# Router logits from extra columns of the qkv and out layers, norm3 no longer turned, out in halves, new step numbers

## The reference

```python
# x [64, 32, 512], ctx [64, 257, 512], 16 heads of 32
x = x + xattn(_layernorm(x), ctx)          # softmax attention over 257 rows, then @ W_out.T + b_out
x = x + attn(_layernorm(x))                # q, k, v by low-rank layers with a rotation, 32 x 32 per batch, then @ Wo_w + Wo_b
x = x + ffn(_layernorm(x))

def ffn(x):                                # E = 8 experts, H = I = 512
    logits = xf @ Wg + bg
    idx = argmax(softmax(logits))
    h = gelu(einsum('th,ehi->tei', xf, W1) + b1)
    y = einsum('tei,eih->teh', h, W2) + b2
    return y[token, idx[token]]
```

## Time and profile before

| | |
|---|---|
| median of 3 runs | 849.17 us |
| profiled execution | 850.44 us |
| its span | 848.6 us |
| busy share | PE 88%, DVE 69%, ACT 52%, POOL 38% |
| first part with batches | to about 606 us |
| tail, to the first gather of the expert part | about 606 to 665 us |
| expert part | about 665 to 848.6 us |

### The profile page before, as it was taken

The page is one execution under the profiler, slowest core; times in us unless marked ns, Lnnn a source line. Parts: engine busy times, 40 slices in busy tenths (PEclk is TensorE's granted clock), DMA queues, the critical chain, the costliest instruction groups (busy, mean ns, idle before and its releaser), DMA issues.

```text
span 848.6 us, 26125 instructions
## 1 busy us (share of the span) xinstructions
PE 745.6 (88%) x10442; PEld 552.9 (65%) x10442; DVE 584.1 (69%) x1163; ACT 440.4 (52%) x1095; POOL 323.7 (38%) x638
## 2 busy tenths in 40 slices
PE   5997878989899898988989889898888779999998
PEld 3544756768677685776857667586676646666664
DVE  3467677777767777777777777767535646788883
ACT  2343475564655656556465655646422335555552
POOL 2113453342523424243242432424310444876642
PEclk9998999999899999999999999999998899999999
DMA  9953764665645565465654546442231599554430
GB/s 275 325 151 67 152 158 122 153 149 115 169 115 139 146 144 145 130 152 137 151 139 137 152 120 168 140 114 89 92 133 51 180 372 363 171 161 141 145 114 4
DMA packets 113848, 129.05 MB, mean 152 GB/s; under 512 B 13950, under 2 KB 80766, under 8 KB 113728
## 3 DMA queue, kind: packets, MB, share of 16 engines
q1 hardware_dynamic: 105984, 109.26, 46.8%
q0 software_dynamic: 5520, 16.26, 5.6%
q10 hardware_dynamic: 2224, 1.86, 0.8%
HBM read 114.76 MB, written 14.42 MB: 152 GB/s over the span
## 4 chain that ended last, share of the span: by engine, by line
PE 66%; DVE 9%; POOL 8%; ACT 7%; issue 6%; DMA 4%; SPq 0%; DVEq 0%; POOLq 0%; ACTq 0%
PE bank L507 11%; PE bank L509 9%; PE bank L508 9%; PE bank L1561 7%; PE scores L548 5%; PE bank L572 5%; PE bank L501 4%; PE scores L558 3%; ACT prob L823 3%; POOL operand_lo L1293 2%; PE bank L704 2%; PE scores L1539 2%; PE scores L1541 2%; PE scores L1540 2%; DMA k_block<-in_L_attn_Wu_v_w 2%
## 5 line engine op out<-in xcount | busy, mean ns | idle before, releaser
L823 ACT ACTIVATE prob<-scores,negmax 128x257 f32<-128x257 f32 x256 | 118.2, 477 | 26.4 <-DVE negmax L1031 25.7
L507 PE MATMUL bank<-qkv_hi,operand_hi 128*128 128x396 f32 x256 | 96.0, 375 | 0.0
L1031 DVE TENSOR_REDUCE negmax<-scores 128x2 f32<-128x514 f32 x128 | 82.0, 682 | 15.5 <-PE scores L548 15.5
L1021 DVE STREAM_TRANSPOSE k_t<-keys 128x512 f32<-128x512 f32 x128 | 87.8, 689 | 2.9 <-DMA keys<-in_ctx 2.9
L508 PE MATMUL bank<-qkv_lo,operand_hi 128*128 128x396 f32 x256 | 88.5, 346 | 0.0
L509 PE MATMUL bank<-qkv_hi,operand_lo 128*128 128x396 f32 x256 | 88.0, 344 | 0.0
L1561 PE MATMUL bank<-w_all,hidden 128*128 x184 | 82.8, 593 | 0.6 <-ACT hidden L1614 0.6
L572 PEld LDWEIGHTS bank<-prob_t,context 128*32 128x32 f32 x4096 | 46.6, 115 | 54.1 <-issue 46.6
L558 PE MATMUL scores<-consts,prob 128*128 128x128 f32 x512 | 74.8, 278 | 4.8 <-ACT prob L823 4.7
L1275 POOL COPY plast<-prob 128x2 f32<-128x2 f32 x128 | 24.7, 193 | 129.8 <-ACT prob L823 129.7
L1657 DVE TENSOR_TENSOR w_lo<-w_all,w_hi 128x512 fp32r<-128x512 f32 x89 | 71.6, 863 | 1.8 <-ACT w_hi L1593 1.7
(11 more groups left out here) (244 smaller groups left out, 1671.4 us busy)
## 6 DMA issues: line engine op xcount, KB each, us to landing
keys<-in_ctx SPq DMA_DIRECT2D x256, 128.0 KB, 4.4
context<-in_ctx SPq DMA_DIRECT2D x64, 512.0 KB, 4.6
w_all<-in_L_ffn_W SPq DMA_DIRECT2D x16, 1024.0 KB, 12.1
b<-in_L_ffn_b SPq DMA_DIRECT2D x23, 256.0 KB, 3.5
norm_scratch<-norm SPq DMA_DIRECT2D x16, 256.0 KB, 2.0
x_tile<-in_x SPq DMA_DIRECT2D x8, 256.0 KB, 5.5
x_pair<-in_x SPq DMA_DIRECT2D x8, 256.0 KB, 5.5
x_scratch<-x_tile SPq DMA_DIRECT2D x8, 256.0 KB, 3.0
```

Source lines behind the costliest of these rows:

```text
L507: pe.matmul(to, op_hi[op][:, c, :], w_hi[name][:, c, columns], start=(c == 0), stop=False)
L823: act.activation(prob[pair][:, gg, :], scores[:, g, 0:J], ACT.Exp, bias=negmax[b % 2][:, g:g + 1], accum_out=sums[t % 2][:, g, bl:bl + 1]) ...
L1021: dve.transpose(dst, src).then_inc(keys_turned, 1)
L1031: dve.tensor_reduce(negmax[b % 2][:, 2 * pair:2 * pair + 2], scores[:, 2 * pair:2 * pair + 2, 0:J], AX.X, ALU.max, negate=True).then_inc(m ...
```

## The change

- The layer norm before the router is folded: the router's weights are centred (their mean over the inputs taken off), so that a logit is (x2 @ centred Wg) / std + bg. x2 is x1 plus the out layer, and x1 @ centred Wg is the second norm's product times its std. So the qkv layer gets 8 columns more (`GATE_AT`, 398 in place of 396 per product), the out layer 8 more (Wo @ centred Wg).
- 520 columns do not fit a bank of 512, so out goes in two halves of 260 columns in two banks (`out_part`): 24 products in place of 12.
- TURN3, X3_MOVE and GATE are gone. CHOOSE starts from `gate_sum` (DVE, 8 columns, ahead of X2) and `rstd_r`. POOL gets three small operations per tile (`std_s`, `gate_x1` twice).
- Six set-up units are new: `center`, four `turned` (Wo turned) and `gate`.
- Nearly all step numbers are new, some banks too.

```diff
-AV, SELF_HI, SELF_LO, OUT, X2, ROOT3 = 66, 66, 70, (81, 85, 86, 87), 89, 85
-SCALE3, TURN3, X3_MOVE, GATE, CHOOSE, RANK, RANKED = 90, 95, 96, 105, 105, 120, 120
+AV, SELF_HI, SELF_LO, OUT, X2, ROOT3 = 63, 73, 71, (86, 88, 92, 94), 96, 99
+SCALE3, CHOOSE, RANK, RANKED = 104, 104, 120, 118
+GATE_KEEP = 43
...
-LATER = {'OUT': (16, -4), 'X2': (19, 0), 'SCALE3': (26, 12), 'TURN3': (29, 7), 'GATE': (38, 14), 'CHOOSE': (31, 4), 'RANK': (25, 1)}
+LATER = {'OUT': (11, -11), 'X2': (2, -3), 'SCALE3': (20, 12), 'CHOOSE': (11, 14), 'RANK': (26, -7)}
...
-QKV_W = 3 * D + ROT
+GATE_AT = 3 * D + ROT
+QKV_W = GATE_AT + E
...
+        def out_part(c):
+            hi, lo = out_weights(w_hi, c), out_weights(w_lo, c)
+            for half in range(2):
+                pe.matmul(out_pair[:, half, 0:HALF + GH], op_hi[OP_SELF][:, c, :], hi[:, half, :], start=(c == 0), stop=False)
+            for half in range(2):
+                pe.matmul(out_pair[:, half, 0:HALF + GH], op_hi[OP_SELF][:, c, :], lo[:, half, :], start=False, stop=False)
+            for half in range(2):
+                done = pe.matmul(out_pair[:, half, 0:HALF + GH], op_lo[OP_SELF][:, c, :], hi[:, half, :], start=False, stop=(c == G - 1))
+            return done
...
+            if kind == "center":
...
+                for g in range(G):
+                    done = pe.matmul(bank[:, 0:E], tables[:, P:2 * P], wg[:, g, :], start=(g == 0), stop=(g == G - 1))
+            if kind == "turned":
...
+                for k in range(G):
+                    done = pe.transpose(bank[:, k * P:(k + 1) * P], staged_a[:, k, c * P:(c + 1) * P], ident)
+            if kind == "gate":
...
+                for o in range(G):
+                    for k in range(G):
+                        pe.matmul(bank[:, o * E:(o + 1) * E], wo_t[:, k, o * P:(o + 1) * P], wg[:, k, :], start=(k == 0), stop=(k == G - 1))
+                for k in range(G):
+                    done = pe.matmul(bank[:, G * E:(G + 1) * E], tables[:, P:2 * P], wg_bias[:, k, :], start=(k == 0), stop=(k == G - 1))
...
-                done = dense_part(OP_SELF, c, "out", slice(0, D), bank)
+                done = out_part(c)
...
-            t = tile_at(step, TURN3, LATER["TURN3"])
-            if t >= 0:
-                bank = bank_for("norm3", t)
-                until.wait_ge(normed_r, t + 1)
-                turn(norm3, bank, norm3_turned)
-            t = tile_at(step, GATE, LATER["GATE"])
...
-                    done = pe.matmul(bank[:, 0:E], x3[:, g * P:(g + 1) * P], wg[:, g, :], start=(g == 0), stop=(g == G - 1))
...
+                until.wait_ge(gate_kept, t + 1)
+                until.wait_ge(gate_used, t)
+                dve.tensor_tensor(halves(gate_sum[:, :]), halves(gate_x1[t % 2][:, :]), out_pair[:, :, HALF:HALF + GH], ALU.add)
+                dve.tensor_tensor(halves(x_tile[t % 4][:, :]), halves(x_tile[t % 4][:, :]), out_pair[:, :, 0:HALF], ALU.add).then_inc(x2_made, 1)
...
-                dve.tensor_tensor(logits[:, :], banks[bank_of["gate"]][:, 0:E], bias_g[:, :], ALU.add).then_inc(gate_used, 1)
+                dve.scalar_tensor_tensor(logits[:, :], gate_sum[:, :], rstd["r"][:, :], bias_g[:, :], ALU.mult, ALU.add).then_inc(gate_used, 1)
```

More of the change, by code:

```diff
@@ L222, in program @@
     last_t, last_p = sba("last_t", [P, G, B]), sba("last_p", [P, G, B])
-    bias_xout, bias_out, bias_v = (sba(n, [P, D]) for n in ("bias_xout", "bias_out", "bias_v"))
+    bias_xout, bias_out = (sba(n, [P, D]) for n in ("bias_xout", "bias_out"))
+    bias_v = sba("bias_v", [P, D + E])
     bias_qk = sba("bias_qk", [P, 2, D])
     bias_g = sba("bias_g", [P, E])
-    wg = sba("wg", [P, G, E])
-    widths = (("xout", D), ("qkv", QKV_W), ("out", D))
+    wg, wg_bias, out_bias = sba("wg", [P, G, E]), sba("wg_bias", [P, G, E]), sba("out_bias", [P, G])
+    gate_c, gate_sum, std_s = sba("gate_c", [P, E]), sba("gate_sum", [P, E]), sba("std_s", [P, 1])
+    gate_x1 = [sba(f"gate_x1_{i}", [P, E]) for i in range(2)]
+    widths = (("xout", D), ("qkv", QKV_W), ("out", D + E))
     w_hi = {n: sba(f"{n}_hi", [P, G, w], F32R) for n, w in widths}
@@ L232, in program @@
     norm_x, norm_w, norm3 = (sba(n, [P, D]) for n in ("norm_x", "norm_w", "norm3"))
-    soft, x3 = sba("soft", [P, D]), sba("norm3_t", [P, D])
+    soft = sba("soft", [P, D])
     qk = sba("qk", [P, 2, D])
[L236 to L239, removed]
+    late = sba("late", [P, 6 * D + 2 * E])
+    att_w, soft_t, q2_t = (late[:, i * D:(i + 1) * D] for i in range(3))
+    v_w = [late[:, i:i + D + E] for i in (3 * D, 4 * D + E)]
+    last_w = late[:, 5 * D + 2 * E:6 * D + 2 * E]
     k_block = sba("k_block", [P, G, BT, HL, S])
@@ L385, in program @@
     emptied = {"queries": queries_placed, "xout": x1_made, "norm": norm_lo, "q": q2_moved, "self": soft_shifted, "av": self_lo,
-               "out": x2_made, "norm3": x3_moved, "gate": gate_used, "rank": rank_used}
+               "out0": x2_made, "out1": x2_made, "rank": rank_used}
     last_bank = banks[(bank_of["queries"] + 1) % 3]
@@ L516, in bank_for @@
             elif t == 0:
-                until.wait_ge(bias_moved, 4)
-                until.wait_ge(weight_lo, CUTS.index(("v", G - 1)) + 1)
+                for n in range(len(UNITS) - 3, len(UNITS)):
+                    until.wait_ge(*emptied_unit(n))
             if before is not None:
@@ L808, in set_up @@
                 cut(w_hi["qkv"][:, c, K_AT:K_AT + D], staged_d[:, c, :])
+            if kind == "turned":
+                until.wait_ge(unit_done, n + 1)
+                act.activation(wo_t[:, c, :], bank[:, :], ACT.Copy).then_inc(wo_turned, 1)
+            if kind == "gate":
+                until.wait_ge(unit_done, n + 1)
+                cut(gate_columns(w_hi), bank[:, 0:G * E].rearrange("p (c h e) -> p c h e", c=G, h=2))
         def move_prob(b, pair):
@@ L949, in scalar_program @@
                 until.wait_ge(staged_a_loaded, 32)
-                cut(w_hi["out"][:, step - OUT_CUT_AT, :], staged_a[:, step - OUT_CUT_AT, :])
+                cut(out_weights(w_hi, step - OUT_CUT_AT)[:, :, 0:HALF], halves(staged_a[:, step - OUT_CUT_AT, :]))
+            if step == GATE_CUT_AT:
+                until.wait_ge(centered, 1)
+                cut(w_hi["qkv"][:, :, GATE_AT:QKV_W], wg[:, :, :])
             stages(step)
@@ L1318, in stages @@
             if t >= 0:
+                until.wait_ge(gate_used, t)
                 root("r", measured_r, t + 1, normed_r, rstd_r)
+            t = tile_at(step, GATE_KEEP)
+            if t >= 0:
+                until.wait_ge(qkv_moved, 4 * t + 4)
+                until.wait_ge(x2_made, t - 1)
+                until.wait_ge(weight_lo, len(CUTS))
+                until.wait_ge(pool_own, own.count)
+                a = own.done(pool.tensor_scalar(gate_x1[t % 2][:, :], v_w[t % 2][:, D:D + E], std_s[:, :], None, ALU.mult))
+                until.wait_ge(pool_own, a)
+                pool.tensor_tensor(gate_x1[t % 2][:, :], gate_x1[t % 2][:, :], gate_c[:, :], ALU.add).then_inc(gate_kept, 1)
+        pool.memset(bias_v[:, D:D + E], 0.0).then_inc(zeroed, 1)
         pool.memset(running[:, :], 0.0).then_inc(zeroed, 1)
@@ L1457, in attention_over @@
         until.wait_ge(rank_done, T)
-        until.wait_ge(x3_moved, T)
+        until.wait_ge(normed_r, T)
         until.wait_ge(dve_own, ranked)
```

145 lines of the change are left out of this document (85 added, 60 removed).

## The result

The changed kernel takes 841.68 us (median of 5 runs, 837.98 to 842.70) against 849.17 before. The ratio is 0.990, with a 95% interval of 0.988 to 0.993: some 7.5 us faster, where 829 us, 20 less, was forecast. The profiled execution took 840.57 us, its span is 838.4 (before 850.44 and 848.6), so 10.2 us of span have to be found.

What follows compares the result with a forecast made beforehand. PE was taken to bound the kernel, with waits on chains through other engines. Tiles -21, set-up +3, tail -5, late delivery +3 sum to -20 from 850.44: 830, or 829 us on the median's scale; range 809 to 851.

Steps and rivals of the forecast that it cites:

- The price of the narrow product: Out layer on PE: a product of 260 columns takes 0.12 us, bounds 0.11 and 0.18.
- rival (2): Out layer: weight load not hidden, 0.23 us per narrow product, 1.6 us per tile, 854 us; chance 0.08.
- The undisturbed tile: Middle tile without a clock dip: three PE stretches sum to 33.0 us, 2.17 less than 35.17.
- Q to S0: PE from the first qkv product to the first batch's scores issued: 17.51 us falls to 15.95.
- S0 to S1: PE from first batch's scores issued to second batch's: 8.98 us falls to 8.25.
- S1 to `norm_w`: PE from second batch's scores issued to the turn of `norm_w`: turns at 6.9 us.
- the walk: The prediction's method: following the new instruction order through a tile's three PE stretches to cost the change.
- The dips: Middle tiles: granted clock falls ahead of `norm_w` in every tile, not one in two, 1.28 us each.
- The late delivery: SP's loads of x and keys, behind the later third norm: 0 to 1 us per tile, 0.2 taken, +3.
- rival (3): SP's queue becomes the bound: keys or x two microseconds late per tile, 28 us, 857 us; chance 0.1.
- Set-up: New units before the first tile's xout: 7.0 us of PE work, between 0 and +7, +3 taken.
- Tail: Last tile: logits about 3.5 us after the statistics, shorter PE chain; together -5 us, bounds -3 and -6.

Runs made afterwards that it cites:

- D: Changed kernel with keys issued ahead of the load of x and five idle PE products per tile ahead of `norm_w`: 825.92 us, ratio 0.971.
- A: Changed kernel with the keys of the batch after next issued on SP ahead of the load of x: 831.17 us, ratio 0.977.
- C: Changed kernel with five idle PE products per tile in the waits ahead of `norm_w`, keys left late: 838.77 us, ratio 0.986.
- B: Kernel before the change, with keys issued ahead of the load of x: 850.07 us, ratio 0.998.
- F: Kernel before the change, with idle products ahead of norm3's turn (2), the gate products (1) and the turn of `norm_w` (1): 845.73 us, ratio 0.995.
- E: D with only two idle products per tile, one before the second batch's first turn and one before its attend: 824.84 us, ratio 0.969.
- G: D with the softmax's exponent moved behind the move of the turned probabilities in ACT's queue: 830.27 us, ratio 0.975.
- H: Changed kernel with only 5 of the 20 products of the set-up unit `gate`, logits incomplete: 836.94 us, ratio 0.983.
- I: D with four idle products in the wait ahead of the set-up unit `gate`: 823.14 us, ratio 0.967.
- L: K with six idle products in the one wait left ahead of the unit `gate`: 822.62 us, ratio 0.965.
- K: D with the last set-up units placed some steps earlier: 825.67 us, ratio 0.971.
- J: I with one more idle product behind each fourth product of the unit `gate`, 4 in all: 825.31 us, ratio 0.970.

## Why the prediction missed

The sign was right and the size wrong: 10 us of span gained against 20. Step by step:

- **The price of the narrow product** (0.12) was right, and rival (2) wrong (its own sum gives 14 x 1.6 = 22 and not 25). The Trainium skill (TensorE: Matmul & The Clock Gate, Part 3, "The mechanism") states that PE pulls a weight load ahead of running products when it goes to a row group that does not conflict or to the background weight buffer. The trace agrees in that no load adds to the 0.12 us here; which of the two cases it is, no run shows.
- **The undisturbed tile** was forecast at 33.0 and is 33.65 (D): Q to S0 right (15.95, measured 16.00), S0 to S1 8.25 against 8.48, S1 to `norm_w` 6.9 against 7.10, from there to Q 1.9 against 2.07. This mis-sized sum is the largest part of the miss: 0.65 per tile, 8.5 us over 13. The waits came where the walk had them (the attend at S0 + 5.4 and S1 + 5.1), but PE's work behind them was priced too low: two xout parts take 1.57 in place of 1.4 (the first product of each 0.32, not 0.23), attend and turn 0.80 for 0.7, attend, turn and AV 1.98 for 1.8.
- **The dips** were forecast in every tile, 1.28 each. The price about holds (1.2 to 1.6, once 2.2), the number does not: seven of the tiles 2 to 14 dip. This gives back some 0.5 per tile.
- **The late delivery was the step that failed in its mechanism.** The walk put the keys' arrival at S1 + 13, and there they come. But it put DVE's need at S1 + 13 too, and it is S1 + 10.3: the statistics of x and a low part, which stood between the maxima and the keys before, now stand behind. So I took 0.2 us per tile for what is 0.5 (below); A gains 0.8 (34.8 against 34.0), since it also has two dips fewer. This is rival (3), given 0.1; it gave 2 us per tile, but where the clock dips DVE does not wait for keys, so the two don't add, and where dips are taken away (C) the keys take over.
- **Set-up** (+3) was mis-sized: +4.8, although all else up to there had become somewhat faster (the first exponents of tile 1 start 3.9 us earlier). This stretch varies by 4 us from profile to profile: `norm_w` of tile 2 starts at 154.7, 158.7 and 154.9 in the kernel before, B and F, and at 159.5 to 163.6 in the changed kernel, A, C, D, E and G, so the two groups are apart, but not by a figure as sharp as 4.8. The interval behind, in which the gate unit stands, is 9.5 longer. The 0.11 per record was taken from rows at 2.4 GHz; at 1.2 GHz it is 0.213. H gives 6.7 of the 9.5 to three quarters of the unit.
- **Tail** (-5) and logits after 3.5 us: right, -4.5 and 3.55.

Together for tiles 2 to 15, counted from the intervals between first exponents in the trace after: five with a wait for keys are 35.24, 33.99, 35.24, 35.32 and 34.96, together 6.4 us above five times 33.67 (the undisturbed tile), or 0.5 per tile over 13; seven with a dip are 34.9 to 35.9, together 10.5 above. 13 x 33.67 + 6.4 + 10.5, less 2.2 for the last, shorter round, is the 452.4 of the table.

What the change is worth by itself is seen where neither stands in its way: 33.65 in D against 35.17 of an undisturbed tile before, 1.5 us per tile, 20 us over 13. Of these, 6.4 were not lost in the layers that changed but in an order on SP that nobody had touched, and some 2 in more or dearer dips (10.5 against about 8.5 before). No run parts the folded layers from the new step numbers, so how much of the 1.5 each of them gives stays open.

The clock: PE stood idle 1.0 and 1.4 us with one short turn between, and in half of the tiles the clock fell; 0.9 us of idle products there kept it up (E). The Trainium skill (TensorE: Matmul & The Clock Gate, Part 1, "HAM oscillation — how this bites in real kernels") tells of a loop whose waits on DMAs lower the clock again in each round. The trace agrees that waits in a loop bring the low clock back, here waits on ACT, but in seven rounds of 13 and not in each. What decides which tile dips stays open.

## What to carry to other kernels

When an instruction is moved back, look at every queue in which something waits for it, and date both the arrival and the need of what stands behind it from the new order; the need had moved here as much as the arrival. When two causes can hold a stage at the same level, taking away one shows only a part: test each alone and both together. Count set-up products at the clock that the idle time ahead of them leaves.

## What the runs showed of the hardware

- Two idle products of 256 columns per tile, in waits of 0.96 and 1.44 us, are enough to keep the granted clock full through twelve tiles (E), and three more change nothing (D). Without them five tiles dip (A).
- 32 records of 8 columns take 3.49 us at 2.4 GHz and 6.82 at 1.2, though the engine streams only 8 columns in each. The weight loads (PEld) are busy 1.98 and 2.00 of 2 us in the windows at either clock, so it is they that set the pace, and they slow down with the clock.
- Idle products ahead of a stretch of narrow records let the clock fall later and for a shorter time (some 3.5 us in I, 10 in L, against 13.5 in D and K), they do not take the fall away; more of them between the records don't either (J).
